# Measuring tokens one stage ahead, a rewritten thought stage, and a mixture fed and emptied choice by choice

## What is computed

```python
x = x + L0_xattn(layernorm(x), ctx)     # 16 small heads
x = x + L0_ffn(layernorm(x))            # gated, hidden activations kept 2 of 4
x = x + L1_xattn(layernorm(x), ctx)     # 16 heads of 128, q and k rms-normalised
x = x + L1_ffn(layernorm(x))            # "thought"
x = x + L2_xattn(layernorm(x), ctx)
x = x + L2_ffn(layernorm(x))            # mixture: 64 experts, 6 chosen, 2 shared
x = x + L3_xattn(layernorm(x), ctx)
x = x + L3_ffn(layernorm(x))            # 32 experts of 96, 8 chosen, limited capacity
```

```python
x_norm = layer_norm(x, in_gamma, in_beta)
thought = x_norm[:, -1, :] @ agg_w + agg_b
for _ in range(4):
    t = layer_norm(thought, pn_gamma, pn_beta)
    t = gelu(t @ d1_w + d1_b)                 # 256 -> 1024
    thought = thought + (t @ d2_w + d2_b)     # 1024 -> 256
said = (thought @ bc_w + bc_b)[:, None, :]
out = layer_norm(x + sigmoid(x @ gate_w + gate_b) * said, out_gamma, out_beta)
```

## Time and profile before

| | us |
|---|---|
| median of 3 runs | 2213.2 (2208.67 to 2220.01) |
| the profiled execution's own time | 2205.61 |
| its span | 2203.8 |
| busy: PE, DVE, ACT, Pool | 1990.5, 1501.1, 1153.5, 680.0 |
| mean granted TensorE clock | 0.946 of full speed |
| thought stage | 816.9 to 899.7 |
| mixture | 1245.9 to 1602.5 |
| of it: one-hots, shared units, blocks, end | 1279.8, 1302.0, 1356.8, 1578.0 (starts) |

### The profile page before, as it was taken

How to read it: one execution, slowest core, us unless ns; L and a number is a source line. 1 busy time by engine, 2 the same in 40 slices (tenths; PEclk the granted TensorE clock), 3 DMA queues, 4 the chain that set the end, 5 groups by cost and what they waited for, 6 DMA issues and landing times. The chain is left out here.

```text
span 2203.8 us, 43113 instructions
## 1 busy us (share of the span) xinstructions
PE 1990.5 (90%) x13031; PEld 1704.7 (77%) x13031; DVE 1501.1 (68%) x4244; ACT 1153.5 (52%) x2626; POOL 680.0 (31%) x1298
## 2 busy tenths in 40 slices
PE   6799696989999977799999875999879999988998
PEld 3544485779999973699999765999769999976887
DVE  7788476757878883888888762322268888875565
ACT  4655444756766642566666401444246666653333
POOL 4322102023333310333443164544323333312221
PEclk9899898999999996899999887999989999988999
DMA  2258202011221104610000034999810000014441
GB/s 68 44 113 214 97 1 72 3 72 54 79 70 61 72 25 132 222 49 0 0 0 0 29 109 146 317 316 316 282 38 23 14 21 14 15 32 122 117 115 40
DMA packets 145273, 193.66 MB, mean 88 GB/s; under 512 B 45100, under 2 KB 113300, under 8 KB 142232
## 3 DMA queue, kind: packets, MB, share of 16 engines
q1 hardware_dynamic: 120440, 152.92, 23.1%
q0 software_dynamic: 7632, 20.85, 2.5%
q10 hardware_dynamic: 17072, 18.29, 2.4%
HBM read 169.86 MB, written 56.62 MB: 103 GB/s over the span
## 5 line engine op out<-in xcount | busy, mean ns | idle before, releaser
L2653 DVE COPY l2f_x_t<-bank 128x256 f32<-128x256 f32 x111 | 47.0, 424 | 152.5 <-PE bank L2376 150.9
L2518 POOL DMA_INDIRECT l2f_y_rows<-l2f_y,l2f_target x111 | 111.6, 1006 | 122.5 <-ACT l2f_y L2486 120.1
L713 ACT ACTIVATE l1a_prob<-l1a_masked,l1a_shift,l1a_q_scale 128x512 f32<-128x512 f32 x128 | 104.5, 816 | 76.3 <-DVE l1a_shift L771 74.1
L713 ACT ACTIVATE l3a_prob<-l3a_masked,l3a_shift 128x512 f32<-128x512 f32 x128 | 92.7, 724 | 78.5 <-DVE l3a_shift L775 75.7
L713 ACT ACTIVATE l2a_prob<-l2a_masked,l2a_shift 128x512 f32<-128x512 f32 x128 | 92.8, 725 | 77.5 <-DVE l2a_shift L775 74.7
L2388 PE MATMUL bank<-l2f_x_t,l2f_w 128*128 128x128 f32 x888 | 117.4, 275 | 0.4 <-DVE l2f_x_t L2653 0.4
L1337 ACT ACTIVATE l0a_prob_t<-bank 128x512 f32<-128x512 f32 x128 | 76.2, 599 | 64.3 <-PE bank L1275 63.6
L2388 PEld LDWEIGHTS bank<-l2f_x_t,l2f_w 128*128 128x128 f32 x888 | 108.0, 192 | 0.6 <-issue 0.6
L1354 DVE TENSOR_REDUCE l0a_coarse<-bank 128x32 f32<-128x512 f32 x128 | 87.5, 688 | 26.0 <-PE bank L1265 24.3
L765 DVE CUSTOM_DVE_ANT_0 l3a_masked<-bank,l3a_side 128x512 f32<-128x512 f32 x128 | 88.4, 691 | 14.1 <-issue 12.8
L765 DVE CUSTOM_DVE_ANT_0 l2a_masked<-bank,l2a_side 128x512 f32<-128x512 f32 x128 | 88.4, 691 | 11.2 <-issue 9.9
(11 more groups left out here) (605 smaller groups left out, 7448.1 us busy)
## 6 DMA issues: line engine op xcount, KB each, us to landing
l2f_w<-w_rows SPq DMA_DIRECT2D x111, 304.0 KB
l1a_side<-rms SPq DMA_DIRECT2D x16, 1024.0 KB, 4.8
l2f_x_rows_of<-x_slots ACTq DMA_DIRECT2D x111, 128.0 KB
w_rows<-in_l2f_w SPq DMA_DIRECT2D x4, 2048.0 KB
l2f_hots<-l2f_y_rows SPq DMA_DIRECT2D x8, 768.0 KB, 10.0
l3f_raw<-in_l3f_w SPq DMA_DIRECT2D x24, 256.0 KB, 3.9
l3f_mix<-shares SPq DMA_DIRECT2D x16, 384.0 KB, 3.6
l2f_w_rest<-in_l2f_w SPq DMA_DIRECT2D x111, 48.0 KB
```

The lines of the kernel that those rows point to most:

```text
L713: act.activation(prob[:, unit, :], masked[:, unit, :], ACT.Exp, bias=shift[:, unit:unit + 1], scale=q_scale[:, slot, t:t + 1] if qk_norm e ...
L2518: pool.indirect_dma_start(y_rows, bass.IndirectOffsetOnAxis(target[:, b:b + 1], 0), y[:, b % of.Y_SLOTS, :], None).then_inc(y_stored[b % o ...
L2653: dve.tensor_copy(x_t[:, b % 2, :], turn_bank[b % 2][:, 0:D]).then_inc(x_kept, 1)
```

## The change

**Norm.** The statistics move into buffers of the whole kernel. A class `Ahead` measures two tiles at a time at the end of the stage before (three such takes in the output, sparse, heads and mixture stages, four in the thought stage); the next stage measures only tiles 6 and 7, beside tile 3, and the second heads stage none. Transposes go over four banks (three in the thought stage).

**Query and key stage.** ACT issues the load of the query weights after norm tile 1 and makes the key weights' high part after tile 4.

**Thought stage.** The thought stays in PSUM, once as columns and once as rows; the step's norm is applied behind the hidden product, as a correction by the moments; the biases come in by products; loads have several semaphores, and small ones are issued by ACT. Gates stand between the hidden product and the turn of the Gelu, with one product head in each of steps 3 and 4. The said rows come from products with broadcast columns. DVE multiplies gates 0 and 1, Pool the others. Four takes follow the last write of `x`.

**Mixture.** Shared units 6 to 11 and the output of pairs 0 and 1 move between the one-hot products (DVE's counterparts six one-hots later). Pool scatters choice 5 of all tiles first, choice 0 last, with a semaphore each. Blocks 0 to 4 run one at a time, block b as soon as choices 5 to 5 - b have landed; their row loads and those of blocks 5 to 10 are issued by SP. The output is read back by choice: choice k once blocks - k blocks are stored, 1 MB each, the last in four pieces. DVE adds choices 5, 4 and 3 for all tiles, PE sums 2, 1 and 0 in eight banks.

```diff
-            wait_for(pe, self.kept, t - 1)
+            wait_for(pe, self.kept, t + 1 - len(self.banks))
...
+class Ahead:
...
+    def take(self, dve, n):
+        m = self.m
+        for t in (2 * n, 2 * n + 1):
+            last = dve.bn_stats(m.stats[:, t, :], m.x[:, t, :])
+        last.then_inc(self.stats_done, 1)
+        dve.wait_ge(self.stats_done, n + 1)
+        for t in (2 * n, 2 * n + 1):
+            last = dve.bn_aggr(m.moments[:, t, :], m.stats[:, t, :])
+        last.then_inc(self.moments_done, 1)
+        dve.wait_ge(self.moments_done, n + 1)
+        at = slice(2 * n, 2 * n + 2)
+        dve.tensor_scalar(m.spread[:, at], m.moments[:, at, 1], Norm.EPS, None, ALU.add).then_inc(self.spread_done, 1)
...
+    def invert(self, pool, sets):
+        m = self.m
+        for n in range(sets):
+            at = slice(2 * n, 2 * n + 2)
+            pool.wait_ge(self.spread_done, n + 1)
+            pool.tensor_tensor(m.rstd[:, at], m.spread[:, at], m.minus_half[:, at], ALU.pow)
...
@@ rms_stage, scalar
-                act.wait_ge(k_loaded, 16)
-                act.copy(wk_high[:], wk[:]).then_inc(high_done, 1)
-                norm.scalar(act)
+                norm.scalar(act, after=split_keys)
...
@@ heads_stage, vector
+                    if head is None and k >= 1:
+                        dve.wait_ge(x_added, 2 * (pair - 4))
+                        ahead.take(dve, k - 1)
...
@@ thought stage, tensor, in a step
+                    gate_products(step_tiles(n))
+                    for h in range(sum(BEHIND[:n]), sum(BEHIND[:n + 1])):
+                        products.tensor(pe, h)
                     pe.wait_ge(active_done, n + 1)
...
@@ thought stage, vector, in a step
+                    link(dve.scalar_tensor_tensor(centred[:], minus_sums[:], moments[:, 0:1], hidden_bank[:, 0:span], ALU.mult, ALU.add))
+                    dve.wait_ge(rstd_done, n + 1)
...
+                    dve.scalar_tensor_tensor(hidden[:], centred[:], rstd[:], offsets[:], ALU.mult, ALU.add).then_inc(hidden_set, 1)
...
@@ grouped_mixture
+    shared_out_at = {1: 0, 3: 1}
+    shared_in_at = {8 + 5 * n: of.EARLY * of.SHARED + n for n in range(shared_units - of.EARLY * of.SHARED)}
...
+                for b in range(of.AHEAD):
+                    sp.wait_ge(x_placed[chosen - 1 - b], 16 * TT)
+                    load_rows(sp, b)
...
+                for k in reversed(range(chosen)):
+                    stored = blocks - k
+                    for n in range(of.Y_SLOTS):
+                        sp.wait_ge(y_stored[n], 16 * len(range(n, stored, of.Y_SLOTS)))
+                    if k:
+                        sp.dma_start(y_of[:, k, :, :], returns[:, :, k, :]).then_inc(returned[k], 16)
...
-                turn(0)
-                turn(1)
-                up(0)
-                for b in range(blocks):
+                for b in range(of.AHEAD):
+                    turn(b)
+                    up(b)
+                    down(b)
+                turn(of.AHEAD)
+                turn(of.AHEAD + 1)
+                up(of.AHEAD)
+                for b in range(of.AHEAD, blocks):
...
-                for t in range(TT):
-                    for k in range(chosen):
+                for k in reversed(range(chosen)):
+                    for t in range(TT):
```

642 lines of the change are left out of this document (386 added, 256 removed).

## The result

The changed kernel takes 2233.65 us, the median of 6 runs (2223.72 to 2234.55), beside 2213.39 for the kernel before in as many (2208.67 to 2220.01). The ratio is 1.0079, with a 95% interval of 1.0055 to 1.0103: 0.8% slower. 2165.7 was predicted and the range ended at 2194. The profiled execution took 2234.22 us with a span of 2232.3; PE's line of the page reads

A forecast was written before the change was run, and what follows sets the result against it. PE, busy 90% of the 2203.8 us span, was taken as the bound, so only its idle or low-clock stretches could shrink. 6.0 + 5.5 + 12 + 17 + 7 = 47.5 us gave 2165.7; range 2140 to 2194.

The forecast's parts named there:

- Measuring ahead: Stage starts and ends: normalising starts earlier, less the takes and powers added at the ends; +6.0 us, from -5 to +12.
- Query and key: Query and key stage: norm tiles no longer wait behind the key weights, first key product near 364; +5.5 us, 3 to 6.8.
- Thought: Thought stage: shorter step chain (8.3 us for 9.9), earlier first Gelu, less work after the last; +12 us, 3 to 19.
- Mixture, start: Before the blocks: shared units fit among the one-hots, blocks 0 to 4 done beneath the scatters; +17 us, 7 to 19.
- Mixture, end: After the blocks: reading back by choice starts five blocks earlier, last adds and takes end at 1595.5; +7 us, 3 to 10.
- The early blocks stall: Rival, 0.22: PE's results reach ACT late during x scatters, so blocks 0 to 4 run after them; 17 less, 2183.
- Slower: Rival, 0.04: late hops outlast the x scatters because y scatters go on, block 5 40 us late; 2223.
- PE bounds the one-hots: Rival, 0.08: one-hot products at half clock last to 1335, early blocks start late; 10 less, 2176.
- Steps as long: Rival, 0.14: thought steps don't shorten, gates and heads delaying the Gelu's transposes; thought gives 3, total 2175.
- hidden anyway: Rival, 0.07: the moves happen but loads gate the starts and reads slow each other; half of all terms, 2189.

The follow-up runs named there:

- e12: The changed kernel as it is, on a chip of the other kind, without the stall: 2179.87 us against 2201.56 for the kernel before, ratio 0.990.
- e5: The kernel before the change with a Pool pause (memset of 128 x 512) after each scatter of x: 2219.85 us against 2201.44 without it.
- e2: The changed kernel with a Pool pause (memset of 128 x 512) after each scatter of x, scatters 1.78 us apart: 2202.23 us.
- e16: The changed kernel with 128 x 128 pauses, no measuring ahead at the mixture's end, all returned choices added by DVE: 2169.97 us, ratio 0.9829 to the kernel before.
- e3: The changed kernel with shared units 6 to 11 and the first two pairs' outputs put back behind the one-hot products: 2212.58 us.
- e4: The changed kernel with no early blocks: blocks 0 to 4 wait for all scatters of x: 2215.54 us.
- e15: The changed kernel with no pause, no measuring ahead at the mixture's end, all returned choices added by DVE: 2217.82 us, ratio 1.0038 to the kernel before.
- e7: The changed kernel with at most three scatters of x in flight, no pause: 2180.04 us.
- e9: The changed kernel, at most three scatters of x in flight, no measuring ahead at the mixture's end, DVE adding all returned choices: 2196.45 us against 2209.23, ratio 0.9943.
- e10: The kernel before the change with at most three scatters of x in flight: 2206.75 us, ratio 0.9995.
- e1: The changed kernel without measuring ahead from the mixture to the last heads stage (no takes or powers at the mixture's end): 2222.11 us.

## Why the prediction was wrong

**Measuring ahead, +6.0.** It gave 3.2, about half: the 20.4 us outside the mixture, less 7.9 and 12.8 of the next two terms, plus 3.5 at the mixture's start. The starts gave what was said (first stage 1.0, route 3.4 for 2.4, mixture 3.5 for 2.9). The second heads stage gained 0.5 and not 3.1 net, and the sparse stage lost 2.3 where I had +1.1; takes and powers cost 2.5 in the first heads stage, for 1.6, and nothing that shows in the last one and the output stage.

**Query and key, +5.5** (7.9): right in mechanism. **Thought, +12** (12.8): right in sum by errors that cancel. Its three periods shrank by 9.4 us together where I took 4.8; I had put steps of 6.5 at the upper end. The first Gelu comes 3.4 us earlier for 4.5. From the last Gelu to the stage's end it is 29.7 us as before, where I had 2.5 less.

That the terms outside the mixture add up to 20.4 for 20.6 is therefore partly luck: there measuring gave 3.4 too little, and the other two gave 3.2 too much.

**Mixture, start, +17: this step failed.** It said of the one-hots "I take the phase's end at 1312, PE-bound", and of blocks 0 to 4 "so they are done". On a chip without the stall both are true (e12: one-hots done 31.5 us after the first, where I had 32). On the chip of the comparison the term is -38.0. Even where nothing stalls the 17 holds only against a baseline with late reads: against the profile of the kernel before it is 16.9, but on a chip F that kernel has none. By e5's rows, block 5 turns 14.4 us after the last scatter's start there; with the last scatter at 1344.08 that gives 1358.4, 6.3 us before the 1364.7 of the profile. So some 10.6 are left on a chip F, an estimate. The size 17 had an error of its own: I put block 5's turn before at 1366.7, and it is at 1364.71, because the second turn follows the first at once. I had the lateness of the earlier trace rows in hand and gave it to a rival as a danger to the early blocks alone, while the change moved six units with a hop from PE to ACT, the very kind that was late there, into PE's queue among the one-hots. What stood behind each late unit had been nothing but the next unit; now it is DVE's multiply, the rest of the one-hots, and behind them the shared units' end and the blocks. The reason I gave for sparing them, that gapless PE work shows no such lateness, came from the loop, where Pool scatters every 1.98 us; the one-hots of before, with 1.3 to 1.77, had no shared unit among them that could have shown it. I even let the scatters end later for the longer one-hots. They end earlier, 61.3 us after the first for 64.4, at 1.27 apart. e2 and e16 show that this interval decides.

The early blocks, which I took at 4 us each, need 3.6 at a clock of 1.00 (e3, e12) and 5.63 behind the stall at a clock of 0.54. What I left out is that the rows of block 5 stand in SP's queue behind weights that wait for the early blocks: 31 us from block 0 to block 5. e4 is 18 us shorter without early blocks.

**Mixture, end, +7: this failed as well**, by -13.9, on any chip (-11.8 on e12's, against the 24.3 of before). The reads were sized nearly right: in e2 they have landed 17.0 us after the last scatter's start, where I had 15.1. What I took for the rest, 2.2 us, is 11.7: 16 products per choice at a low clock, with the first sum added only 10.5 us after the first product, and takes between the adds. I had read that PE waits through most of the 24.5 us at the end, but rows 1 has it busy for 13.76 of them; these products were the work that had to follow the reads. And the prediction had no term for Pool's drain, 9.4 us, because before it lay beside the reads and the views don't count it.

**The sum on a chip F.** e12 is 21.7 us faster than before (2179.87 beside 2201.56). 20.4 outside the mixture (if it is as on L), 3.3 + 16.9 - 0.8 - 11.8 in it give 28.0, against the profile of the kernel before, which is of a chip L. On a chip L that kernel has its own, smaller stall in the chain of the earlier trace rows. On chips F it is some 10 us faster (2201.4 and 2201.6, against 2209.2 to 2213.4 on L), and the 6.3 us estimated above are part of that: less these, 21.7 are left, as measured. The kernel before has no profile without a pause on a chip F, so this is an estimate and not shown.

**The rivals.** "The early blocks stall" had the mechanism, with the wrong victims. "Slower" wanted late hops beyond the x scatters; they ended 8 us after the last x scatter, so it was not that. "PE bounds the one-hots" is refuted: 36.7 us for all of it in e12, clock 0.92. "Steps as long" and "hidden anyway" are refuted by the table. The rival that was missing: lateness of 18 and 26 us, priced for every hop that the change puts beneath the scatters. Six units at 6 us each, a third of the smaller one, are 36 us, most of the 47.5 of the forecast.

**What stays open.** What holds the signals up. Of the 12 profiles on chips L, 10 have late signals and two, with a pause, have none; of the 7 on chips F none has any, with or without a pause. The stall shows in issue (PE 2.80 us an instruction without a wait) and in PE's signals to ACT; Pool's own pace and, from 1281.74 on, SP's row issues are untouched. By the Trainium skill (SBUF — State Buffer, Who interferes with whom) PE and ACT never wait on anyone for a port; nothing in these rows speaks against that, and it leaves the ports out. Whether recording a profile takes part I can't say from runs that are all recorded in the same way; but the times that the ratios rest on differ between the kinds of chip as the profiles do. Nor do the rows show why the clock stays low in the early blocks of the changed kernel and not in those of e3. Not tried: the short pause without DVE's adds on a chip L, e15 and e16 on a chip F, and DVE's multiplies behind all one-hots, which would take the late reads out of PE's way.

## What to carry to other kernels

A wait that the profile shows and cannot name is a price for whatever is moved beside it: count the hops that the change adds there and multiply, before calling them hidden, and look whether the change alters the pace of what runs beside them. Put nothing on a queue behind which the end of a stage waits without asking how long that queue drains, above all Pool's behind indirect scatters. And run the uncured kernel on the same chip as the cure (e7 looked like one until e9 and e12). The version to keep is e16, 1.7% faster than the kernel before on a chip with the stall.

## What the runs showed of the hardware

- On some chips, indirect scatters issued by Pool every 1.27 us (128 rows of 1 KB) go with late signals between the other engines: ACT reads PE's products up to 53.6 us late, where 0.04 us is usual, and PE issues one instruction per 2.80 us. SP's waits for the scatters' landings end in time meanwhile. At 1.46 us and above there is no stall (e16; 1.78 in e2), and on other chips not even at 1.27 (e12). Three in flight at most doesn't end it (e9: 33.3 us) and changes nothing in the kernel before (e10).
- Pool's drain at the end of the stage with indirect scatters lasts 9.1 to 9.6 us beyond its last work in all 19 profiles, whether that is a scatter (before, e1) or a power of 0.70 us, 28 us after the last scatter (after). In other stages it ends within 0.1 us of the work.
- The chip matters to a change like this: the same program is at 1.0079 of the kernel before on one and at 0.990 on another, each outside the other's interval.
